# A decoder on one core: linear attention's addition to x moved one step on, and its decay product cut in two halves

## The reference, cut to what matters

```python
x = x + _L1_attn_ref(_layernorm(x, axis=-1), ...)

q = jax.nn.silu(q)
k = jax.nn.silu(k)
q = _lrpe_rotate(q)
k = _lrpe_rotate(k)
scores = jnp.einsum('bthd,bshd->bhts', qi, ki) * D[None]
o_intra = jnp.einsum('bhts,bshd->bthd', scores, vi)
gate = x @ Wg1 @ Wg2
o = _gated_group_rmsnorm(o, gate, norm_weight)
return o @ Wo
```

## Time and profile before

| What | Value |
| --- | --- |
| Median of three runs | 1222.44 us |
| Lowest and highest run | 1220.46 and 1223.41 us |
| The profiled execution: its own time | 1228.56 us |
| Its span in the trace | 1226.7 us |
| TensorE busy in the span | 1141.5 us, 93% |
| VectorE, ScalarE, GpSimd busy | 774.5, 562.1 and 603.1 us |
| Mean granted TensorE clock | 0.98 |

### The profile page before, as it was taken

The page is one execution under the profiler, slowest core; times in us unless marked ns, Lnnn a source line. Parts: engine busy times, 40 slices in busy tenths (PEclk is TensorE's granted clock), DMA queues, the critical chain, the costliest instruction groups (busy, mean ns, idle before and its releaser), DMA issues.

```text
span 1226.7 us, 26308 instructions
## 1 busy us (share of the span) xinstructions
PE 1141.5 (93%) x8174; PEld 886.4 (72%) x8175; DVE 774.5 (63%) x1938; ACT 562.1 (46%) x1502; POOL 603.1 (49%) x751
## 2 busy tenths in 40 slices
PE   7998999978999789988999999999997999999996
PEld 5776666644555434477887888888886879999995
DVE  4555688867888679975776676777666643222221
ACT  3444777852333200035666666666665652222221
POOL 2102566635655457754566666666564523323323
PEclk9999999989999889999999999999998999999999
DMA  7000000006999040030000000000001138888884
GB/s 286 1 0 9 15 15 15 11 2 133 186 195 179 1 178 1 4 137 2 6 14 14 14 14 17 13 13 21 13 14 52 53 110 230 243 238 240 239 233 97
DMA packets 57272, 99.88 MB, mean 81 GB/s; under 512 B 5809, under 2 KB 44017, under 8 KB 56433
## 3 DMA queue, kind: packets, MB, share of 16 engines
q1 hardware_dynamic: 42432, 62.92, 20.6%
q10 hardware_dynamic: 7616, 26.74, 6.0%
q0 software_dynamic: 7152, 9.34, 4.3%
HBM read 87.53 MB, written 30.48 MB: 96 GB/s over the span
## 4 chain that ended last, share of the span: by engine, by line
PE 51%; DMA 14%; issue 12%; DVE 8%; ACT 5%; POOLq 4%; POOL 4%; DVEq 2%; ACTq 0%
DMA out<-g.spare,ex.token 13%; PE bank L2231 9%; PE bank L2119 8%; PE bank L2144 4%; PE bank L2128 3%; PE bank L512 2%; PE bank L2195 2%; PE bank L1184 2%; PE bank L1355 2%; PE bank L1356 2%; PE bank L2137 2%; PE bank L1357 2%; PE bank L1251 1%; PE bank L1242 1%; ACT ga.e L1987 1%
## 5 line engine op out<-in xcount | busy, mean ns | idle before, releaser
L2119 PEld LDWEIGHTS bank<-ga.xnT,g.early 128*128 128x128 f32 x1280 | 153.1, 195 | 7.7 <-issue 7.7
L2119 PE MATMUL bank<-ga.xnT,g.early 128*128 128x128 f32 x1280 | 158.4, 278 | 0.0
L1744 POOL TENSOR_TENSOR ga.halves<-ga.halves,g.ga_sinT 128x512 f32<-128x512 f32 x80 | 103.4, 1292 | 62.3 <-ACT ga.halves L1980 62.3
L2231 PE MATMUL bank<-g.early,ga.aT 128*128 128x256 f32 x512 | 117.0, 382 | 0.5 <-ACT ga.aT L2002 0.5
L1987 ACT ACTIVATE ga.e<-bank,ga.negmax 128x128 f32<-128x128 f32 x256 | 90.4, 366 | 50.9 <-DVE ga.negmax L1841 49.9
L1752 POOL TENSOR_TENSOR ga.kqT<-ga.by_cos,ga.halves 128x512 f32<-128x512 f32 x80 | 102.4, 1280 | 16.0 <-issue 16.0
L2231 PEld LDWEIGHTS bank<-g.early,ga.aT 128*128 128x128 f32 x512 | 94.9, 190 | 12.3 <-ACT ga.aT L2002 0.7
L1828 DVE TENSOR_TENSOR ga.by_cos<-bank,g.ga_cosT 128x512 f32<-128x512 f32 x80 | 55.2, 691 | 68.1 <-PE bank L2119 49.4
L2360 DVE TENSOR_TENSOR g.spare<-g.spare,bank 128x512 f32<-128x512 f32 x39 | 26.8, 688 | 97.6 <-PE bank L2417 93.2
L2144 PE MATMUL bank<-ga.pT,ga.v 128*128 128x512 f32 x128 | 69.2, 623 | 14.1 <-ACT ga.pT L1995 13.8
L2408 PEld LDWEIGHTS bank<-g.spare 128*128 128x128 f32 x624 | 75.6, 192 | 1.9
(11 more groups left out here) (311 smaller groups left out, 2621.5 us busy)
## 6 DMA issues: line engine op xcount, KB each, us to landing
g.spare<-in_mo_w SPq DMA_DIRECT2D x39, 512.0 KB, 4.3
g.spare<-in_mo_w ACTq DMA_DIRECT2D x39, 512.0 KB, 4.7
mo_rows<-in_pad_rows SPq DMA_DIRECT2D x1, 18447.0 KB, 109.0
g.spare<-mo_rows SPq DMA_DIRECT2D x39, 129.0 KB, 3.2
g.late<-in_mo_w SPq DMA_DIRECT2D x1, 4096.0 KB, 13.6
g.ctxT<-in_ctxR SPq DMA_DIRECT2D x1, 2048.0 KB, 13.7
xa.ctxT<-in_ctxT SPq DMA_DIRECT2D x16, 128.0 KB, 2.6
g.spare<-cv_rows SPq DMA_DIRECT2D x1, 2048.0 KB, 8.0
```

Source lines behind the costliest of these rows:

```text
L1744: nc.gpsimd.tensor_tensor(by_sin[:, par, :].rearrange("p (h t) -> p h t", h=REP), halves[:, par, :].rearrange("p (h t) -> p h t", h=REP), ...
L2119: last = nc.tensor.matmul(pkq[:, par, j * P:(j + 1) * P], w[:, q, at * P:(at + 1) * P], xnT[:, s.par, q, :], start=(q == 0), stop=(q == C ...
L2231: last = nc.tensor.matmul(pout, aT[:, h // REP, (h % REP) * P:(h % REP + 1) * P], g.ga_wo[:, h, :], start=(h == 0), stop=(h == H - 1))
```

## The change

On VectorE the addition of `pout` to x leaves the end of step s, where it took sequence a, and stands behind `u` at the start of the next step, where that sequence is c. The decay product becomes two instructions, each over one half of the heads (half k of the columns in each of the four banks), and each signals `a_ready`; the counts of those who wait for it double. On TensorE a function `masked_values(b, k)` does the eight matmuls of one half; half 0 now stands ahead of the transposes of `un`, half 1 behind them. Nothing is computed differently. Cross-attention's code is the same in both files.

```diff
--- before.py
+++ after.py
@@ -1041,6 +1041,9 @@
                 dve.wait_ge(gate_ready, upto(a))
                 nc.vector.scalar_tensor_tensor(out=u[:], in0=gate[:, a.par, :], scalar=1.0, in1=pon,
                                                op0=ALU.add, op1=ALU.mult).then_inc(u_ready, 1)
+            if c.on:
+                dve.wait_ge(out_done, upto(c))
+                nc.vector.tensor_tensor(g.x[:, c.i, :], pout, g.x[:, c.i, :], ALU.add).then_inc(x_added, 1)
             if b.on:
                 dve.wait_ge(qk_turned, upto(b))
                 if b.past(2):
@@ -1076,8 +1079,10 @@
                     dve.wait_ge(av_done, upto(b, back=2))
                 elif not b.past(1):
                     dve.wait_ge(xa.pv_done, B)
-                nc.vector.tensor_tensor(a_mat[b.par], ps[:].rearrange("p r n -> p (r n)"),
-                                        g.la_decay.rearrange("p h t -> p (h t)"), ALU.mult).then_inc(a_ready, 1)
+                for k in range(C):
+                    nc.vector.tensor_tensor(a_mat[b.par].rearrange("p (r k n) -> p r k n", r=4, k=C)[:, :, k, :], ps[:, :, k * D:(k + 1) * D],
+                                            g.la_decay.rearrange("p (r k h) t -> p r k (h t)", r=4, k=C)[:, :, k, :],
+                                            ALU.mult).then_inc(a_ready, 1)
             if a.on:
                 dve.wait_ge(norm_ready, upto(a))
                 if a.past(1):
@@ -1098,9 +1103,6 @@
                 if n.past(2):
                     dve.wait_ge(xn_ready, upto(n, back=2))
                 layer_norm_stats(nc, m, g.x[:, n.i, :], n.par, var_ready)
-            if a.on:
-                dve.wait_ge(out_done, upto(a))
-                nc.vector.tensor_tensor(g.x[:, a.i, :], pout, g.x[:, a.i, :], ALU.add).then_inc(x_added, 1)
         return Part(step, 2, 3)
 
     def scalar(act):
@@ -1161,6 +1163,16 @@
             pe.wait_ge(g.fill, 4)
             pe.wait_ge(xa.exp_done, 2 * B)
 
+        def masked_values(b, k):
+            pe.wait_ge(a_ready, upto_part(b, C, k))
+            for q in range(2):
+                for r in range(4):
+                    at, head = q * 256 + (k * 4 + r) * 32, (r * 2 + k) * 2 + q
+                    last = nc.tensor.matmul(po[32 * r:32 * r + 32, k, :],
+                                            vd[:, b.par, :, :].rearrange("p q y -> p (q y)")[:, at:at + 32],
+                                            a_mat[b.par][:, head * P:(head + 1) * P], start=(q == 0), stop=(q == 1))
+            return last
+
         def step(s):
             a, b, c, n1 = s.back(2), s.back(1), s.back(3), s.back(-1)
             if b.on:
@@ -1189,7 +1201,7 @@
                 pe.wait_ge(kT_ready, upto(b))
                 pe.wait_ge(qT_ready, upto(b))
                 if b.past(1):
-                    pe.wait_ge(a_ready, upto(b, back=1))
+                    pe.wait_ge(a_ready, upto(b, back=1, per=C))
                 else:
                     pe.wait_ge(xa.oT_ready, B)
                     pe.wait_ge(xa.o_ready, B)
@@ -1223,6 +1235,9 @@
                 last.then_inc(turned, 1)
             if s.base is None and s.n == B + 1:
                 s.meet()
+            if b.on:
+                pe.wait_ge(v_ready, upto(b))
+                masked_values(b, 0)
             if a.on:
                 pe.wait_ge(un_ready, upto(a))
                 if s.on:
@@ -1233,16 +1248,7 @@
                     last = nc.tensor.transpose(pun[:, k * P:(k + 1) * P], un[:, k * P:(k + 1) * P], g.ident[:])
                 last.then_inc(un_turned, 1)
             if b.on:
-                pe.wait_ge(v_ready, upto(b))
-                pe.wait_ge(a_ready, upto(b))
-                for k in range(C):
-                    for q in range(2):
-                        for r in range(4):
-                            at, head = q * 256 + (k * 4 + r) * 32, (r * 2 + k) * 2 + q
-                            last = nc.tensor.matmul(po[32 * r:32 * r + 32, k, :],
-                                                    vd[:, b.par, :, :].rearrange("p q y -> p (q y)")[:, at:at + 32],
-                                                    a_mat[b.par][:, head * P:(head + 1) * P], start=(q == 0), stop=(q == 1))
-                last.then_inc(av_done, 1)
+                masked_values(b, 1).then_inc(av_done, 1)
             if a.on:
                 pe.wait_ge(unT_ready, upto(a))
                 if n1.on:
@@ -1347,7 +1353,7 @@
             head = u % H
             if u == 0:
                 pe.wait_ge(g.filt_loaded, 16)
-                pe.wait_ge(la.a_ready, B)
+                pe.wait_ge(la.a_ready, C * B)
             pe.wait_ge(g.kv_ready, u + 1)
             if u >= 2:
                 pe.wait_ge(z_ready, u - 1)
```

## The result

The changed kernel took 1215.61 us (median of 16 runs, 1211.99 to 1222.08) beside 1224.51 us for the kernel before (16 runs, 1220.46 to 1226.38): a ratio of 0.994, with a 95% interval of 0.9928 to 0.9953, so some 7.3 us less, 5.8 to 8.8 by the interval (the two medians lie 8.9 us apart; I go by the ratio). It is faster. The profiled execution took 1215.25 us with a span of 1213.4 (before: 1228.56 and 1226.7).

What follows compares the result with a forecast made beforehand. Waits in linear attention bound it: circle A at 9.33 us, then circle B at 9.08. Steps gave 2.25 us, the stage's end 0.8, taken as 3.1: 1222.4 to 1219.3 us; range 1216.9 to 1221.8, its own 1218.2 to 1220.6.

Steps and rivals of the forecast that it cites:

- Circle A: Linear attention's wait loop through `u`, scores, decay product, `un`, values and projection: 9.33 us a step, forecast to shrink to 8.9.
- Circle B: Linear attention's wait loop `un`, rotation, `qkr`, transposes, `qT`, statistics, root, next `un`: 9.08 us, limiting second steps to 9.09.
- The rival of a tighter circle B: In the loop, hand-over 0.13 and root 3.03 us make second steps 9.27, first ones 9.53; total 1221.0 us; chance 0.23.
- The tie with VectorE's own pace: In the loop, VectorE's own instructions from `qT` to `un` and circle B's root path both take 5.34 us.
- The halves at 0.07 us: Splitting the decay product on VectorE into two instructions costs 0.07 us more per step, bounds 0 to 0.16.
- Alone it would have no such cover: Between `u` and `qT`, the moved addition is covered (`u` 0.2 us inside its 2.95 limit) only because the values were halved.
- the stage: Linear attention, first `u` to last addition to x; step gains and its end summed to 3.05 us, taken as 3.1.
- The end of the stage: Last linear attention steps, from `un` at 423.14: half the values leave the way to `u`, saving 0.8 us in all.
- Behind this stage convolution, attention and experts hang on its end, and move with it: Later convolution, attention and experts shift with linear attention's end; the saving, taken as 3.1 us, carries to the median.
- The clock did not stay up: Rival: at the end of linear attention TensorE's clock holds, some 2 us come back, total 1217.3 us; chance 0.17.
- No half was held by GpSimd: Rival: GpSimd's `la.norm` holds the decay product's second half, `un` comes 1.14 us later, total 1236 us; chance 0.04.
- Nothing gained: Rival: additions and halves only refill waits, linear attention's end included; total 1222.4 us, give or take 1; chance 0.06.

## Why the prediction was right or wrong

**Circle A shrinks and no longer binds: right.** L1196 follows L1189 by 0.22 us, as forecast, and `u` comes 2.81 us behind `un`, forecast 2.75, inside the limit of 2.95. The first half of the values went into the gap ahead of `un`'s transposes.

**Circle B takes over at 9.09: right, to 0.04.** Its pieces measured 3.72 (forecast 3.74), 2.40 (2.39), 2.91 and 0.03 (0.04), and the step 9.05. The rival of a tighter circle B (9.27) fell: the hand-over to `qT` is 0.04, and the root takes 2.91 in the loop. The tie with VectorE's own pace was right too: halving the root bought 0.08 us in a second step and nothing in a first one.

**The halves at 0.07 us: right**, 0.05 measured with the root out of the way. The Trainium skill's rule on the flush ("VectorE: DVE Perf Modes", "The DRAIN you can't avoid"), by which they would have cost 0.16, does not bear on them: instructions that wait for nothing started 0.08 us ahead of the end of the one before them, here as in the kernel before. The same section has that exception (an operation that isn't held starts earlier), which the prediction left out when it put the page's price at 0.16.

**"Alone it would have no such cover": half right.** With the addition moved alone `qT` came 0.2 us later than with the halves, yet the stage gained 1.4 us. The forecast knew the address work ahead of `cn.stats` but counted it only together with the halves.

**The end of the stage: forecast 0.8, measured 1.07, by the wrong sum.** "`un` at 423.14 waits for the root, nothing saved there" failed: that step lost 0.50 us. The root before had itself waited 0.47 us for the mean square, because `u`, and with it ScalarE's square, came right ahead of `qT`; now `u` is 0.9 us ahead of `qT`, the wait is gone, and the root took 2.91 instead of 3.03. A wait that ends late had a wait behind it, and I followed it one link only. The way from `u` to the next `un` behaved as written: 0.85 us less up to `u`, 0.33 more behind it for the addition, 0.52 left against 0.55 (its own terms, 0.97 - 0.1 - 0.34, give 0.53). The 0.25 us for the last transposes did not come: they stood 0.67 us behind `un`, and 0.72 before.

**The stage: forecast 3.1, measured 3.76.** What is missing is 0.2 in first steps, 0.2 in second ones, where I had 9.09 for 9.05 and took every step at 9.33, and 0.3 at the end. Had the rest stood still, the run would have been at 1218.7, inside its own range.

**"Behind this stage convolution, attention and experts hang on its end, and move with it": this is the step that failed.** They hang on it, but did not merely move. In every profile of every kernel with the halves 1.4 us fell away in one router step, where an idle piece of VectorE's moved and a conversion was no longer held by GpSimd. Some 2 us more lie in places where a small VectorE instruction is held or not, or the granted clock falls or not. The forecast's sum had no term for any of this, in either direction, and its range no room for it. It did know that GpSimd can hold VectorE (`cn.xn`, 1.97 us), but asked that only of the halves.

**The rivals.** The clock did not stay up at the end of the stage (0.50 from 418 to 422), although the median is below the 1217.3 which that case gave: the right side for another reason. No half was held by GpSimd: the second halves start beside the root and take 1.21 us. "Nothing gained" fell.

## What to carry to other kernels

When a circle of waits through several engines is to be cut, write down the next one with its pieces before costing the cut: here the second lay 0.25 us below the first, and gave the step to 0.04 us. Then look for what the remaining bounds share; moving one drain out of their common piece gave 2.6 us of stage for one line. Judge such changes by the distance between landmarks in the trace, which repeats to 0.2 us, and give the run's time a few us of range of its own: added instructions alone can move an idle piece elsewhere in the program, and a shift of a tenth of a microsecond can decide whether VectorE or GpSimd waits for the other. When a tiny instruction takes a microsecond, look at what GpSimd runs beside it.

## What the runs showed of the hardware

A VectorE conversion of 128x2 took 1.22 us instead of 0.17 when it began 0.07 us behind a GpSimd instruction of 1.27 us, and it ended 0.02 us behind that one. The same holds for `ga.negmax` (128x4) and a copy of 128x2, and at the stage's end `cn.xn` (1.97 us) began 0.07 us behind a GpSimd instruction too; it does not hold for the halves of the decay product (1.21 to 1.23 us beside the root). VectorE showed an idle piece of 0.42 to 0.46 us without a wait, whose place in the program changed when five or ten drains, or the halves, were added ahead of it. TensorE's mean granted clock between the roots near 917 and 953 us was 0.95, 0.87 or 0.83 in executions of the two kernels, and the stretch took 35 to 36, 39 and 40 us. GpSimd's root of 128x16 takes 2.91 or 3.03 us and one of 128x8 1.65 or 1.78; from the two lower values I estimate a fixed part of about 0.4 us and 0.16 us for each column, which gives 0.55 for a single column, where `cn.rstd` took 0.55 to 0.58. A drain between `qT` and the statistics behind it cost the statistics' start 0.18 us (0.79 against 0.61), and nothing ahead of `qT`, where VectorE waits 0.16 us for TensorE anyway.
